# The second half of a mixture-of-experts layer written as one block in place of two

## What is computed

```
x = x + attention(layernorm(x))
# feed forward, T = 1024 tokens, H = 512, FFN = 1536
shared_out = (x1 * silu(x2)) @ shared_w2.T          # x1, x2 = halves of xn @ shared_w1.T
w_topk, idx_topk = top_k(softmax(xn @ wg.T), 8)     # 64 experts, weights normalised to sum 1
buf = tokens of each expert, up to 160 rows
out = (x1 * silu(x2)) @ expert_w2.T                 # per expert, x1, x2 = halves of buf @ expert_w1.T
x = x + shared_out + sum over experts of w * out
```

## Time and profile before

| what | value |
|---|---|
| median of 3 runs | 2502.98 us |
| the three runs | 2498.66, 2502.98, 2503.08 us |
| span of the profiled execution, first to last instruction | 2494.3 us |
| median less that span (what lies around it) | 8.7 us |
| PE busy | 2406.8 us, 96% of the span |
| shared expert and routing | about 326 to 554.8 us |
| routed experts | 559.4 us to the end |

### The profile page before, as it was taken

The page is one execution under the profiler, slowest core; times in us unless marked ns, Lnnn a source line. Parts: engine busy times, 40 slices in busy tenths (PEclk is TensorE's granted clock), DMA queues, the critical chain, the costliest instruction groups (busy, mean ns, idle before and its releaser), DMA issues.

```text
span 2494.3 us, 54951 instructions
## 1 busy us (share of the span) xinstructions
PE 2406.8 (96%) x22810; PEld 1959.0 (79%) x22810; DVE 1981.7 (79%) x1894; ACT 1689.3 (68%) x2121; POOL 569.7 (23%) x410
## 2 busy tenths in 40 slices
PE   6779989999999999999999999999999999999998
PEld 4557777778888888888888888888888888888886
DVE  7785667657899899988878989988778878877795
ACT  5553443336888788878777878877667767766784
POOL 0000020002223232332222223322222222212221
PEclk9989999999999999999999999999999999999999
DMA  8760042347999899999988999999888888878894
GB/s 231 217 212 1 3 168 88 112 160 271 360 378 383 325 374 388 384 340 361 343 307 318 386 341 363 371 353 353 285 311 324 322 300 328 324 275 285 328 359 135
DMA packets 129043, 715.08 MB, mean 287 GB/s; under 512 B 15488, under 2 KB 23808, under 8 KB 52928
## 3 DMA queue, kind: packets, MB, share of 16 engines
q1 hardware_dynamic: 103104, 668.06, 69.7%
q0 software_dynamic: 25600, 41.96, 7.9%
HBM read 684.46 MB, written 25.49 MB: 285 GB/s over the span
## 4 chain that ended last, share of the span: by engine, by line
PE 77%; issue 0%; POOL 0%; DVE 0%; ACT 0%; ACTq 0%; POOLq 0%; DVEq 0%
PE ps L1627 14%; PE ps L1629 14%; PE ps L1628 14%; PE ps L1705 7%; PE ps L1707 7%; PE ps L1706 7%; PE ps L1658 5%; PE ps L1677 4%; PE ps L1690 3%; PE ps L1614 1%; PE ps L1668 1%; PE ps L1617 0%; POOL out_rows L1590 0%; POOL out_rows L1588 0%; DVE e_XEl L1541 0%
## 5 line engine op out<-in xcount | busy, mean ns | idle before, releaser
L1519 DVE TENSOR_TENSOR e_WL<-ring,e_WH 128x2048 fp32r<-128x2048 f32 x231 | 528.8, 2289 | 116.9 <-ACT e_WH L1439 114.9
L1519 DVE TENSOR_TENSOR XSl<-ring,XSh 128x2048 fp32r<-128x2048 f32 x229 | 524.1, 2289 | 106.8 <-ACT XSh L1439 104.8
L1439 ACT ACTIVATE e_WH<-ring 128x2048 fp32r<-128x2048 f32 x231 | 442.3, 1915 | 45.6 <-PE ps L1629 27.9
L1439 ACT ACTIVATE XSh<-ring 128x2048 fp32r<-128x2048 f32 x229 | 438.7, 1916 | 47.0 <-PE ps L1629 28.9
L1576 POOL TENSOR_TENSOR e_tick<-e_tick 128x1 f32<-128x1 f32 x126 | 111.9, 888 | 1301.7 <-ACT X L1487 1202.4
L1627 PE MATMUL ps<-e_WH,e_XEh 128*128 128x512 f32 x920 | 361.9, 393 | 0.0
L1629 PE MATMUL ps<-e_WH,e_XEl 128*128 128x512 f32 x920 | 358.6, 390 | 0.0
L1628 PE MATMUL ps<-e_WL,e_XEh 128*128 128x512 f32 x920 | 358.1, 389 | 0.0
L1519 DVE TENSOR_TENSOR e_WL<-e_more,e_WH 128x2048 fp32r<-128x2048 f32 x114 | 260.9, 2289 | 52.0 <-ACT e_WH L1439 51.0
L1627 PE MATMUL ps<-XSh,e_XEh 128*128 128x512 f32 x616 | 243.0, 394 | 4.6 <-DVE e_XEl L1541 4.6
L1629 PE MATMUL ps<-XSh,e_XEl 128*128 128x512 f32 x616 | 240.7, 391 | 0.0
(11 more groups left out here) (243 smaller groups left out, 4602.6 us busy)
## 6 DMA issues: line engine op xcount, KB each, us to landing
ring<-in_experts SPq DMA_DIRECT2D x462, 1024.0 KB
e_more<-in_experts SPq DMA_DIRECT2D x114, 1024.0 KB, 8.3
ring<-in_shared SPq DMA_DIRECT2D x12, 1536.0 KB, 6.2
a_K<-in_ctx_k SPq DMA_DIRECT2D x32, 514.0 KB, 4.9
a_V<-in_ctx_v SPq DMA_DIRECT2D x32, 384.0 KB
a_V<-in_ctx_v SPq DMA_DIRECT2D x32, 130.0 KB
X<-in_x SPq DMA_DIRECT2D x4, 512.0 KB, 5.3
xn_scratch<-ring SPq DMA_DIRECT2D x1, 2048.0 KB, 8.5
```

The costliest lines, as they stand in the source:

```text
L1439: act.activation(halves(nth)[0], unit(i), ACT.Copy).then_inc(hi_done, 1)
L1519: dve.tensor_tensor(l, unit(place(kind, n)), h, ALU.subtract).then_inc(lo_done, 1)
```

## The change

The two blocks become one: the `Block` that opens at the shared expert stays open for the routed experts, so there is no drain and no barrier between them. What the barrier ordered is now ordered by single waits:

- PE transposes the tokens of expert 0 (`first_tokens`) ahead of the last `down`, step 23, instead of behind it. It waits for `gf_done` at 24 there, since bank 2 was read until then.
- DVE does `tokens_low(0)` first and `add_shared(1)` behind it; before, `add_shared(1)` stood ahead of the barrier.
- PE waits for `so_added` at 8 before `over(0)`, because that writes bank 4. ACT waits for the last down product (`dn_done` at 24) before `high(GATE, 1)`, because e_WH lies where d_ tiles were.
- SP waits for `dn_done` at 24 and `lo_done` at 2, loads the units 8 and 9, then waits for `so_added` at 8 and stores the second half of X, and goes on with unit 10. Before, the store stood ahead of units 8 and 9.
- `so_out` becomes two semaphores, one for each half: `silu(0)` waits for the first, `weigh(0)` for the second.
- tick is allocated once, ahead of the other tiles, and its second memset goes. XEh, XEl and XEo come first among the e_ tiles. In the built program every d_ and e_ tile but XEh, XEl, XEo and tick keeps its order and moves, those of the shared expert by 32 bytes.

```diff
-        so_out = sem("so_out")
+        so_out = [sem(f"so_out{i}") for i in range(2)]
+        tick = sb("e_tick", [P, 1])
...
-            block = st.enter_context(nc.Block())
+            block = root.enter_context(nc.Block())
...
+            def add_shared(dve, half):
+
+                dve.wait_ge(dn_done, J * half + J)
+                for t in range(4):
+                    row = 4 * half + t
+                    dve.tensor_tensor(X[:, row, :], X[:, row, :], ps[:, 4 + t, :], ALU.add).then_inc(so_added, 1)
...
-                store_rows(1)
                 sp.wait_ge(zero_out, 32)
...
-                add_shared(1)
...
+                def first_tokens():
+
+                    first_ps, first_over_ps = turned_tokens(0)
+                    pe.wait_ge(gathered[0], 32)
+                    pe.wait_ge(gf_done, 2 * J)
+                    for k in range(G):
+                        pe.transpose(first_ps[:, k * P:(k + 1) * P], XG[:, 0, k * P:(k + 1) * P], ident[:, :])
+                    pe.transpose(first_over_ps, XO[:, 0, :], ident[:, :]).then_inc(xe_psum, 1)
...
+                    if n == 2 * J + LAG - 1:
+                        first_tokens()
                     if n >= LAG:
                         down(n - LAG)
...
-                first_ps, first_over_ps = turned_tokens(0)
-                pe.wait_ge(gathered[0], 32)
-                for k in range(G):
-                    pe.transpose(first_ps[:, k * P:(k + 1) * P], XG[:, 0, k * P:(k + 1) * P], ident[:, :])
-                pe.transpose(first_over_ps, XO[:, 0, :], ident[:, :]).then_inc(xe_psum, 1)
...
+            XEh = sb("e_XEh", [P, 2, G, P], F32R)
+            XEl = sb("e_XEl", [P, 2, G, P], F32R)
+            XEo = sb("e_XEo", [P, 2, G, CAP2])
             more = sb("e_more", [P, MORE * UNIT])
...
-            block = st.enter_context(nc.Block())
-
             @block.sync
             def _(sp):
+                sp.wait_ge(dn_done, 2 * J)
+                sp.wait_ge(lo_done, EARLY)
                 for i in range(RING, 3 * NP):
+                    if i == R:
+                        sp.wait_ge(so_added, 8)
+                        sp.dma_start(out_tiles[:, 4:8, :], X[:, 4:8, :]).then_inc(so_out[1], 16)
...
                     if n == 0:
-                        act.wait_ge(so_out, 32)
+                        act.wait_ge(so_out[0], 16)
...
                     if e >= 1:
                         act.wait_ge(added, 32 * e)
+                    else:
+                        act.wait_ge(so_out[1], 16)
...
                 tokens_over(0)
+                act.wait_ge(dn_done, 2 * J)
                 high(GATE, 1)
...
                 tokens_low(0)
+                add_shared(dve, 1)
                 low(GATE, 1)
...
-                pool.memset(tick[:, :], 0.0).then_inc(ticked, 1)
-
...
-                        pool.wait_ge(so_out, 32)
+                        pool.wait_ge(so_out[0], 16)
+                        pool.wait_ge(so_out[1], 16)
...
                         if n == 0:
+                            pe.wait_ge(so_added, 8)
                             with pe.If(now < 1):
                                 over(n)
```

More of the change, by code:

```diff
@@ L846, in program @@
             kept = sb("d_kept", [P, 2, NE])
-            tick = sb("d_tick", [P, 1])
             XN = ring[:, PAIR:PAIR + TT * D].rearrange("p (t d) -> p t d", t=TT)
@@ L919, in store_rows @@
                     sp.wait_ge(so_added, 4 * half + 4)
-                    sp.dma_start(out_tiles[:, tiles, :], X[:, tiles, :]).then_inc(so_out, 16)
+                    sp.dma_start(out_tiles[:, tiles, :], X[:, tiles, :]).then_inc(so_out[half], 16)
                 sp.dma_start(wgs, wg).then_inc(wg_in, 16)
@@ L1151, in read_lists @@
                     dve.tensor_copy(lists[:, 0, es, :].rearrange("p e w -> p w e"), tok).then_inc(list_ready, 1)
[L1153 to L1158, removed]
                 layernorm(dve, X, XN, mv, small, Tally(dve, ln_done), std_ready, xn_ready)
@@ L1170, in _ @@
                     if n == J + LAG:
-                        add_shared(0)
+                        add_shared(dve, 0)
                     product(n)
@@ L1359, in program @@
             GTl = sb("e_GTl", [P, 2, G, P], F32R)
-            XEh = sb("e_XEh", [P, 2, G, P], F32R)
-            XEl = sb("e_XEl", [P, 2, G, P], F32R)
-            XEo = sb("e_XEo", [P, 2, G, CAP2])
             SLo = sb("e_SLo", [P, P])
@@ L1365, in program @@
             GTo = sb("e_GTo", [P, 2, G, CAP2])
-            tick = sb("e_tick", [P, 1])
             SL = [X[:, i, :] for i in range(2)]
@@ L1403, in program @@
             y2_ready = sem("e_y2_ready")
-            ticked = sem("e_ticked")
             added = sem("e_added")
```

## The result

| | median | runs | range |
|---|---|---|---|
| before | 2503.08 us | 13 | 2498.66 to 2510.78 |
| changed | 2511.10 us | 13 | 2506.88 to 2516.64 |

The ratio of changed to before is 1.0031, with a 95% interval of 1.002 to 1.0042: 8 us slower where 6.3 us faster was forecast, and outside the stated range. The profiled execution of the changed kernel has a span of 2512.2 us.

The account below looks back on a forecast made before the run. PE was taken as the bound; 4.8 us of idle plus 1.6 of clock minus 0.15 of new wait gave 6.25, called 6.3, so 2502.98 us would become 2496.7, range 2492 to 2500.

Parts of the forecast that it names:

- What bounds the kernel: In the routed experts PE is the bound, so an interval cut from PE leaves the total whole.
- The transposes: Moved ahead of the last down product, with XEl's wait hidden, they let gates_of(0) start at 554.6, saving 4.8 us idle.
- The clock: At the first gate product, half clock behind the idle disappears: 1.6 us won, bounds 0 to 2.4.
- The wait at the first branch: Before over(0), PE waits for the adds of add_shared(1): 0.15 us lost, bounds 0 to 0.5.
- ACT, DVE, SP, POOL: After the seam between the blocks, their moved work holds up nothing; DVE reaches product(0) 0.6 us early; cost nothing.
- Moved tiles: Matmuls on d_ and e_ tiles now 32 bytes past a multiple of 64 take no longer: cost nothing.
- slower, by the moved tiles: Rival, 5%: moved tiles slow the experts' 6912 matmuls; 1.6 ns each gives 0.2% slower, 3 ns gives 2517.4 us.
- The sequencer: Rival, 12%: PE's sequencer shows between last down and first gate matmul, up to 1.8 us back; 2498.5 us.
- The rule on transactions off 256 bytes: Rows of 8192 bytes starting off 256 need 33 transactions, not 32: 3% more for e_more units, hidden by SP's waiting.
- The range: For the whole kernel's time, 2492 to 2500 us, from the seam's bounds and run scatter; forecast at 66%.

Follow-up runs that it names:

- e2: The changed kernel with tick 64 columns wide, so d_ and e_ tiles start on multiples of 256 bytes again; 2495.07 us, ratio to before 0.9979.
- e10: The changed kernel with tick placed in the existing one-column tile unused instead of a new tile; 2495.20 us, ratio to before 0.9975.
- e1: The kernel before with one unused column added, d_ and e_ tiles 32 bytes later, no instruction moved; 2516.45 us, ratio to before 1.0059.
- e7: The kernel e2 with only XEh, XEl and XEo 32 bytes late; 2517.37 us, ratio 1.006.
- e9: The kernel e2 with the five transposes put back behind the last down product; 2493.98 us in a single execution.
- e8: The kernel e2 with add_shared(1) put back ahead of tokens_low(0) on DVE; 2502.91 us in a single execution.
- e4: The changed kernel with tick ahead of ring, so ring, XSh and XSl also start 32 bytes late; 2497.35 us, ratio 0.9986.
- e6: The kernel e2 with only XSh and XSl 32 bytes late; 2511.47 us in a single execution.
- e3: The changed kernel with tick 16 columns wide, d_ and e_ tiles 64 bytes past a multiple of 256; 2510.28 us, ratio 1.004.
- e5: The changed kernel with tick 32 columns wide, d_ and e_ tiles 128 bytes past a multiple of 256; 2504.11 us in a single execution.

## Why the prediction was wrong, by its own steps

- **What bounds the kernel** held. PE waits 0.5 us in all between 556 and 2500 us in the changed kernel, and what is taken from PE (e2, e10) or laid on it (e1, e7) shows in the total. This is why 5 ns on a matmul can't hide.
- **The transposes** held: `gates_of(0)` 0.22 us behind the last down matmul, forecast 0.23. XEl had 0.9 us to spare, forecast 0.7. e9 gives this part 1.6 us, e8 the order of the adds 4.8.
- **The clock** held: 1.00 over the first gate product. The reading that the clock falls behind an idle of 4.5 us has more rows now: behind e1's idle of 4.48 us the gate product took 5.39 us at half clock, worse than before's 4.51; behind 3.17 us (e8) it fell as well, and behind 2.52 us in attention too (before: idle from 310.79 to 313.31, half clock from 313.80 to 317.20); behind 1.4 us (e9) it didn't. The bounds of 0 to 2.4 us were fair, 1.6 was one value among them.
- **The wait at the first branch**: 2.98 us from gate to `over`, forecast 3.05. The wait itself can be read: from the last gate matmul's start to `over` pass 0.32 us where the adds are done before that start (before, e8, e9), 0.41 in the changed kernel and 0.49 in e2. So it costs 0.1 and 0.2 us, forecast 0.15. `over` starts 0.30 us behind the adds in both, where 0.38 was borrowed from another place.
- **ACT, DVE, SP, POOL** held. DVE stood 0.95 us before `product(0)`, forecast 0.6, and PE waited for no transfer.
- **Moved tiles: this is the step that failed.** It was costed at nothing, and measures 14 us (the changed kernel against e10): 10.3 in the experts after the seam, and by the estimate above 3.5 in the shared expert. The reason given was that b_XTl with b_WP, both 32 bytes off, takes 389 ns. That row answers another question. In it both operands are off alike, as in e4, which is fast too. In the changed pairs one operand moved and the other (XSh, XSl) stayed, and in the built program of before no large matmul has operands that differ modulo 256. The step looked at each tile's own alignment when it should have gone through the pairs and asked which of them the shift took apart. The unknown should have been bounded from pairs of the kind, and since there were none, left open at a price per matmul, as the rival did.
- **The rival "slower, by the moved tiles"** had the mechanism's place and its sign, at 5%. Its price was spread over all 6912 matmuls at 1.6 ns for a clear loss. In truth 3 x (616 + 308) = 2772 of the experts and 576 of the shared expert pay, and they pay 2 to 6 ns: by the mean distances of the starts 1848 gate and upper matmuls at 6.0 (11.1 us), 924 of the down products at 2.1 (1.9), 576 up matmuls at 5.5 (3.2), less some 1.4 that the down products on e_WH and e_WL gained: 14.8 us, against 14 measured. It deserved far more than 5%, because the only evidence against it didn't bear on it.
- **The sequencer** did not show through. In the changed kernel the read began at 564.4 and the gate product at 567.88; so the sequencer, which has the jump ahead of the read, was 3.5 us early. So the Trainium skill's rule on taken branches ("Runtime: NRT & Kernel Launch", Instruction fetch mechanics) cost nothing visible at this jump. The rule is for a target outside the window that is already fetched, and no row shows whether this target was.

```profile
L1720 PEldq TENSOR_LOAD <-narrow x64: 296/314/1206, 564.4 to 2460.1; - x64
```

- **The rule on transactions off 256 bytes**, from the Trainium skill ("DMA: Bandwidth & Descriptors", How a descriptor splits into AXI transactions), was put at 3% and hidden. The profile's median from issue to landing in e_more is 8.4 us in the changed kernel, and 8.3 in e2, with the tile aligned; but e6, where it is aligned too, has 8.4. No run here separates such a price from scatter.
- **The range** was built around scatter and the seam's bounds, and held no share of an address effect at all. With the forecast at 66% and "slower" at 5%, that is the same fault again.

Left open: why two operands that differ modulo 256 cost 5 to 6 ns of 227. A collision between the load of the next held tile and the stream of the present one is a guess; no run here shows the reads themselves, and it would have to say why `over`'s matmuls pay nothing. Also open is why the down products lose less (2 ns in the mean): with GTh held, the first of three terms stands at 236 ns even where all tiles agree, and only 231 in e7, where no address of this pair changed modulo 256. So something besides the pair's own addresses acts on them.

## What to carry to other kernels

Where PE is the bound, a new tile of one column can be an edit to every large matmul whose tiles lie behind it: go through the pairs of held and streamed operands and see that both still start at the same place modulo 256 bytes, and put small new tiles last, or into a free one. An experiment with nothing but an unused column shows at once whether an unexplained loss is of this kind. And when a row is brought as evidence that a change costs nothing, it has to differ in the same way as the change does; a row in which both operands moved says nothing on one that moved alone. At a seam between two stages, let PE's next operands be made ahead of work that nobody waits for: the order of four adds was worth 4.8 of the seam's 6.3 us.

## What the hardware showed that was not expected

- The fp32r matmuls of 128x512 of the gate, upper and up products start 227 ns apart when held and streamed tile agree modulo 256 bytes, and 232 to 235 ns apart when they differ by 32, 64 or 128 bytes (e1, e3, e5, e6, e7 and the changed kernel slow; e4 fast, with both off alike). The duration of the rows of the second term goes from 389 to between 394 and 397 ns. The down products lose 2 ns in the mean, and float32 matmuls of 128x128 with 32 columns held lose nothing. Other differences, shapes and types were not run.
- After attention, around the end of an idle of 4.5 us (5.5 in e1), the clock was at half for 3.4 to 13.7 us in the profiles of this case, though the code there is the same. This row is of the changed kernel, with PE idle at first, then busy for 12.07 of the 13.70 us and still at 1.2 GHz:

```profile
330.30:344.00 13.70, 12.07 (x56) 11.42 (x56) 8.22 (x18) 6.13 (x10) 6.40 (x7) 0.50 0.81 302
```

- Attention ended between 324.2 and 332.6 us in the 12 profiles, with no edit to it. Single executions of this kernel move by several us with that alone, so a difference of 6 us was settled by rows and by many runs together, not by one of them.
